# A mixture-of-experts kernel: expert outputs stored in the order of the units and gathered per token inside the expert loop

## The reference

```python
x = x + attn(layernorm(x))                          # token mixer, then channel mixer
xt = layernorm(x).reshape(-1, 256)                  # 8192 tokens
gates = sigmoid(xt @ expert_sel.T)                  # 8192 x 32
sel_val, sel_idx = top_k(gates, 4)
scores = relu(einsum('nd,edf->nef', xt, keys))      # 128 numbers per expert
scores = scores * gate_full[:, :, None]             # 0 where the expert was not taken
x = x + einsum('nef,efv->nv', scores, values)
```

## Time and profile before

| what | value |
|---|---|
| median of 3 runs | 1308.65 us (1304.46 to 1309.5) |
| span of the profiled execution, first to last instruction | 1307.0 us |
| mean granted TensorE clock | 0.966 of full |
| PE busy | 1185.3 us (91%) |
| DVE busy | 1030.5 us (79%) |
| ACT busy | 832.7 us (64%) |
| POOL busy | 800.2 us (61%) |
| DMA | 196.98 MB, mean 151 GB/s |

### The profile page before, as it was taken

How to read it: one execution, slowest core, us unless ns; L and a number is a source line. 1 busy time by engine, 2 the same in 40 slices (tenths; PEclk the granted TensorE clock), 3 DMA queues, 4 the chain that set the end, 5 groups by cost and what they waited for, 6 DMA issues and landing times.

```text
span 1307.0 us, 27473 instructions
## 1 busy us (share of the span) xinstructions
PE 1185.3 (91%) x7372; PEld 1030.4 (79%) x7373; DVE 1030.5 (79%) x2462; ACT 832.7 (64%) x1761; POOL 800.2 (61%) x900
## 2 busy tenths in 40 slices
PE   7799999999999999999999875999999999992665
PEld 6678887888788778887878754999999999992444
DVE  4789889888988887898898668777777777771777
ACT  4468567656856765675685562677777777771443
POOL 2523567666866866776675667677777777774000
PEclk9799999999999999999999985999999999995999
DMA  7001112121221212122121287787766666668999
GB/s 229 1 17 33 57 50 90 66 77 53 77 77 49 89 58 76 61 73 81 45 86 58 103 340 258 227 248 236 213 209 211 206 207 204 204 186 296 411 412 355
DMA packets 119841, 196.98 MB, mean 151 GB/s; under 512 B 16368, under 2 KB 92400, under 8 KB 118384
## 3 DMA queue, kind: packets, MB, share of 16 engines
q1 hardware_dynamic: 82672, 114.03, 27.3%
q0 software_dynamic: 26112, 71.86, 15.0%
q10 hardware_dynamic: 11008, 10.52, 2.3%
HBM read 101.09 MB, written 95.26 MB: 150 GB/s over the span
## 4 chain that ended last, share of the span: by engine, by line
PE 57%; DVE 9%; POOL 9%; DMA 8%; issue 8%; ACT 5%; SPq 2%; DVEq 1%; ACTq 0%; POOLq 0%
PE ps L468 18%; PE ps L1559 12%; DMA ye<-expert_rows_spare 5%; POOL lists L1351 4%; PE ps L1547 4%; PE ps L677 3%; PE ps L1540 2%; PE ps L671 2%; PE ps L673 2%; PE ps L1541 2%; PE ps L1542 2%; DMA expert_rows_spare<-y,dest 2%; PE ps L615 2%; ACT kr L770 1%; PE ps L458 1%
## 5 line engine op out<-in xcount | busy, mean ns | idle before, releaser
L1678 POOL DMA_INDIRECT expert_rows_spare<-y,dest x288 | 282.2, 980 | 92.8 <-issue 84.6
L1559 PE MATMUL ps<-xt_hi,keys 128*128 128x128 f32 x1152 | 223.7, 281 | 6.8 <-DVE keys L1628 6.8
L1559 PEld LDWEIGHTS ps<-xt_hi,keys 128*128 128x128 f32 x1152 | 188.2, 194 | 9.3 <-DVE keys L1628 8.8
L1351 POOL DMA_INDIRECT lists<-rows_even,slot x128 | 145.0, 1133 | 42.6 <-issue 38.1
L1351 POOL DMA_INDIRECT lists<-rows_odd,slot x128 | 140.5, 1098 | 41.1 <-issue 39.0
L1559 PE MATMUL ps<-xt_lo,keys 128*128 128x128 f32 x576 | 159.4, 277 | 0.0
L1639 DVE TENSOR_TENSOR xt_lo<-ps,xt_hi 128x512 fp32r<-128x512 f32 x144 | 99.5, 691 | 59.2 <-ACT xt_hi L1592 58.3
L1592 ACT ACTIVATE xt_hi<-ps 128x512 fp32r<-128x512 f32 x144 | 86.3, 599 | 84.6 <-PE ps L1559 79.2
L1628 DVE TENSOR_TENSOR keys<-experts_raw,keys 128x256 fp32r<-128x256 f32 x288 | 108.6, 418 | 14.2 <-issue 8.9
L1589 ACT ACTIVATE keys<-experts_raw 128x256 fp32r x288 | 105.4, 425 | 19.5 <-issue 19.3
L1763 PE MATMUL ps<-ye,gate_diag 128*128 128x256 f32 x256 | 66.1, 404 | 56.4 <-DMA ye<-expert_rows_spare 54.8
(11 more groups left out here) (235 smaller groups left out, 3409.0 us busy)
## 6 DMA issues: line engine op xcount, KB each, us to landing
xr<-lists SPq DMA_DIRECT2D x288, 130.0 KB
ye<-expert_rows_spare SPq DMA_DIRECT2D x32, 1024.0 KB, 21.8
x_sb<-in_x SPq DMA_DIRECT2D x16, 512.0 KB, 3.8
residual<-xp SPq DMA_DIRECT2D x16, 512.0 KB, 4.6
experts_raw<-in_expert_in SPq DMA_DIRECT2D x8, 1024.0 KB, 15.5
resid<-residual SPq DMA_DIRECT2D x4, 2048.0 KB, 13.3
out_dram<-resid ACTq DMA_DIRECT2D x32, 256.0 KB, 11.7
expert_rows_spare<-y,dest POOLq DMA_INDIRECT x288
```

The costliest lines, as they stand in the source:

```text
L1351: pool.indirect_dma_start(lists, bass.IndirectOffsetOnAxis(ap=slot[:, q, n:n + 1], axis=0), rows[q][:, n // TOPK, :], None).then_inc(last_ ...
L1559: mm = pe.matmul(ps[:, H + q % HBANKS, c], keys[:, q, s, half, k * DE:(k + 1) * DE], m[:, q, k, c], start=n == 0, stop=n == 3 * KD - 1)
L1678: pool.indirect_dma_start(expert_rows, bass.IndirectOffsetOnAxis(ap=dest[:, r, s:s + 1], axis=0), y[:, r, s, :], None).then_inc(sent[r], 16)
```

## The change

Units are numbered in the order in which they are opened, over all experts: unit `n` lies at row `128 n` of the lists, whichever expert it belongs to. `route_slots` keeps, for each expert, the end of its open unit and what room is left in it, and opens new units as they are needed; a row's place is so known with its final number, and `place_of` keeps the 4 x 512 places of each tile. A row has 256 numbers (1024 bytes). The lists, 36,864 rows, are cleared with zeros in the mix stage, 2048 rows per transfer; the fills of list ends and the plan of units go, but for a smaller plan (`plan_filled`, `plan_order`, `plan_head`, `plan_later`, `plan_end`): 16 units that are full before the last tile go first, then the others in order.

In the expert loop the products are stored by SP, 7 steps behind the loads, to `sorted_rows` at the unit's own rows. POOL waits until all units that a tile can lie in are stored (tile `t`: the first 8 (t + 3) steps), and gathers the rows of its tokens by `place_of`, 16 indirect transfers per tile, to `ye`. DVE sums the four rows of 128 tokens with their gates into `resid` from step 34 on, two instructions per step, between its other work; SP loads the residual and stores the output per tile of 512 tokens. The hardware loop repeats 16 steps. SP waits for `last_scattered` ahead of step 8. The last phase, with its matmuls, goes.

```diff
-ROW = D + TOPK
+ROW = D
...
+UNIT = P
 RING = 8
-
-UNIT = P
-EARLY = ((N - TILE) * TOPK - E * (UNIT - 1)) // UNIT // (SUB * RING) * RING
 UNITS = -(-((N * TOPK - E) // UNIT + E) // (SUB * RING)) * SUB * RING
+LIST = UNIT
+LIST_ROWS = UNITS * UNIT
+HEAD = SUB * RING
+HEAD_END = HEAD + E
+OPENED = TILE * TOPK // UNIT
+LAG_UNITS = E
...
+STORE_LAG, SUM_LAG = 7, 34
+OPEN_BELOW = (UNIT - 1) / UNIT
+EXPERT_SLOTS = (4, 2, 2, 4, 4, 2)
...
+    sorted_rows = nc.dram_tensor("sorted_rows", (LIST_ROWS, D), F32, kind="Internal").ap()
...
+        def clear(first):
+
+            sp.dma_start(lists[bass.ds(first, OPENED * UNIT), :].rearrange("(p n) d -> p n d", n=OPENED),
+                         zeros[:].unsqueeze(1).broadcast_to([P, OPENED, ROW])).then_inc(zeroed, 16)
+
+        AHEAD = LAG_UNITS // OPENED + 1
+        for n in range(AHEAD):
+            clear(n * OPENED * UNIT)
...
+            if has_next:
+                sp.wait_ge(zeroed, 16 * (t + AHEAD))
+                clear((t + AHEAD) * (OPENED * UNIT))
...
-            dve.scalar_tensor_tensor(rows[p][:, :, D:ROW], expert[:], float(SPACED), out_row[:],
-                                     ALU.mult, ALU.add).then_inc(route_step, 1)
-            after_route(5)
-            dve.tensor_scalar(out_row[:], out_row[:], float(TILE * TOPK), None, ALU.add)
...
-            dve.tensor_tensor(place[:], ps[:, PR, 0:J * E].rearrange("p (j e) -> p j e", j=J),
-                              list_end[:].unsqueeze(1).broadcast_to([P, J, E]),
-                              ALU.add).then_inc(place_ready, 1)
-            dve.wait_ge(place_ready, V + 1)
-            dve.tensor_tensor(list_end[:], ps[:, PR, J * E:(J + 1) * E], list_end[:],
-                              ALU.add).then_inc(rank_used, 1)
...
+            dve.tensor_tensor(count_i[:], ps[:, PR, J * E:(J + 1) * E], room[:], ALU.subtract).then_inc(units_step, 1)
+            dve.tensor_tensor(place[:], ranks, room[:].unsqueeze(1).broadcast_to(at),
+                              ALU.subtract).then_inc(rank_used, 1)
+            after_units(1)
+            dve.tensor_scalar(opened_i[:], count_i[:], UNIT.bit_length() - 1, None,
+                              ALU.logical_shift_right).then_inc(units_step, 1)
+            after_units(2)
+            dve.tensor_copy(opened[:], opened_i[:]).then_inc(units_step, 1)
+            after_units(3)
+            dve.tensor_tensor_scan(upto, zeros[:, 0:E], opened[:], before, ALU.add, ALU.add).then_inc(units_step, 1)
+            settled(rank_used, V + 1)
+            dve.scalar_tensor_tensor(room[:], opened[:], float(UNIT), count_i[:], ALU.mult, ALU.subtract)
+            after_units(4)
+            dve.tensor_tensor(fresh[:], upto, opened[:], ALU.subtract).then_inc(units_step, 1)
+            dve.scalar_tensor_tensor(newest[:], opened[:], 0.0, upto, ALU.is_gt, ALU.mult)
+            after_units(5)
+            dve.scalar_tensor_tensor(jump[:], fresh[:], float(UNIT), unit_end[:], ALU.mult,
+                                     ALU.subtract).then_inc(units_step, 1)
+            after_units(6)
+            dve.scalar_tensor_tensor(over[:], place[:], float(UNIT - 1), jump[:].unsqueeze(1).broadcast_to(at),
+                                     ALU.is_ge, ALU.mult)
+            dve.tensor_tensor(place[:], place[:], unit_end[:].unsqueeze(1).broadcast_to(at),
+                              ALU.add).then_inc(units_step, 1)
+            after_units(7)
+            dve.tensor_tensor(place[:], place[:], over[:], ALU.add).then_inc(place_ready, 1)
+            dve.scalar_tensor_tensor(unit_end[:], newest[:], float(UNIT), unit_end[:], ALU.mult,
+                                     ALU.max).then_inc(units_step, 1)
...
+            dve.tensor_copy(place_of[:, bass.ds(V * (J * TOPK), J * TOPK)], slot_f[:])
...
+            dve.wait_ge(head_counts, 4)
+            dve.tensor_copy(plan_expert[:, 0:P], ps[:, HEAD_BANK, P:2 * P])
+            dve.tensor_scalar(plan_row[:], ps[:, HEAD_BANK, 2 * P:2 * P + HEAD_END], float(UNIT), None,
+                              ALU.mult).then_inc(head_ready, 1)
...
+                settled_on(pool, zeroed, 16 * t)
...
+        def rows_of(b):
+            if isinstance(b, int) and b * SUB < HEAD_END:
+                _, at = nc.values_load_multi_w_load_instructions(
+                    plan_row[0:1, b * SUB:(b + 1) * SUB], engines=(sp.engine,), min_val=0,
+                    max_val=LIST_ROWS - UNIT,
+                    skip_runtime_bounds_check_because="the plan writes all of the table, bounded, ahead of head_ready")
+                return at
+            return [b * BLOCK + s * UNIT for s in range(SUB)]
+
+        def step(i, r, pair):
+            if within(i, 0, NSTEPS):
+                at = rows_of(i)
+                after(sp, x_ready, i - SLOTS + 1)
+                for s in range(SUB):
+                    sp.dma_start(xr[:, r % SLOTS, s, :], lists[bass.ds(at[s], UNIT), :]
+                                 ).then_inc(rows_loaded[r % SLOTS], 16)
+            if within(i, STORE_LAG, NSTEPS + STORE_LAG):
+                b, q = i - STORE_LAG, (r - STORE_LAG) % YS
+                at = rows_of(b)
+                sp.wait_ge(ycopy_ready, b + 1)
+                for s in range(SUB):
+                    sp.dma_start(sorted_rows[bass.ds(at[s], UNIT), :], y[:, q, s, :]).then_inc(y_stored[q], 16)
+            if r % RING == 6 and within(i, 46, NSTEPS):
+                tile, q = 2 * pair + (r - 46) // RING, ((r - 46) // RING) % RS
+                store_tile(tile, q)
+            if r % RING == 0 and within(i, 32, NSTEPS):
+                load_resid(2 * pair + (r - 32) // RING, ((r - 32) // RING) % RS, pair - 2)
+
+        def load_resid(tile, q, nth):
+
+            after(sp, out_stored[q], 16 * nth)
+            sp.dma_start(resid[:, q], residual[bass.ds(tile * TILE, TILE), :].rearrange("(j p) d -> p j d", p=P)
+                         ).then_inc(resid_loaded[q], 16)
+
+        def store_tile(tile, q):
+
+            sp.wait_ge(sum_step, TOPK * J * (tile + 1))
+            sp.dma_start(out[bass.ds(tile * TILE, TILE), :].rearrange("(j p) d -> p j d", p=P), resid[:, q]
+                         ).then_inc(out_stored[q], 16)
+
+        sp.wait_ge(head_ready, 1)
         sp.wait_ge(scattered[0], 16 * NT // 2 * J * TOPK)
         sp.wait_ge(scattered[1], 16 * (NT // 2 - 1) * J * TOPK)
-        for i in range(FILL_RINGS * RING):
+        for i in range(3 * PAIR):
             if i == RING:
-                sp.wait_ge(plan_ready, PLANNED)
-            step(i, i % RING, i // RING)
-            if i % RING == RING - 1:
-                fill(sp, i // RING * FILLS)
-        with sp.Fori(FILL_RINGS, EARLY // RING) as ring:
-            for r in range(RING):
-                step(RING * ring + r, r, ring)
-
-        sp.wait_ge(last_scattered, 16 * J * TOPK)
-        sp.wait_ge(filled, 16 * E)
-        sp.wait_ge(area_cleared, 16 * (LIST_ROWS - OVERFLOW) // UNIT)
-        with sp.Fori(EARLY // RING, NSTEPS // RING) as ring:
-            for r in range(RING):
-                step(RING * ring + r, r, ring)
-        sp.wait_ge(pe_step, LAST_STEP)
-        for n in range(RESID_AHEAD, RESID_PIECES):
-            load_resid(sp, resid, residual, resid_loaded[1], n)
+                sp.wait_ge(last_scattered, 16 * J * TOPK)
...
+        def add(i, r, pair, k):
+
+            if not within(i, SUM_LAG, SUM_END):
+                return
+            G, tile, q, j, nth = group(r, pair)
+            if r % 2:
+                k += 2
+            if k == 0:
+                dve.wait_ge(ye_loaded[j], 16 * TOPK * (tile + 1))
+                if j == 0:
+                    dve.wait_ge(resid_loaded[q], 16 * (nth + 1))
+            else:
+                dve.wait_ge(sum_step, TOPK * G + k)
+            acc = resid[:, q, j, :]
+            gate = gates[:, bass.ds(G, 1), k:k + 1].rearrange("p a b -> p (a b)")
+            dve.scalar_tensor_tensor(acc, ye[:, j, k, :], gate, acc, ALU.mult, ALU.add).then_inc(sum_step, 1)
...
+            add(i, r, pair, 0)
+            if within(i, 0, NSTEPS):
...
-                dve.tensor_tensor(mark[:, r, :, 0:TOPK], xr[:, q, :, D:ROW],
-                                  plan_mark[:, bass.ds(i * SUB, SUB)].unsqueeze(2).broadcast_to([P, SUB, TOPK]),
-                                  ALU.subtract).then_inc(mark_ready, 1)
...
+            add(i, r, pair, 1)
+            if within(i, H_LAG, NSTEPS + H_LAG):
...
-                dve.tensor_reduce(dest[:, r, :], mark[:, r], AX_X, ALU.min,
-                                  apply_absolute_value=True).then_inc(dest_ready, 1)
...
-            settled_on(pool, ycopy_ready, i + 1, dest_ready)
-            for s in range(SUB):
-                pool.indirect_dma_start(
-                    expert_rows, bass.IndirectOffsetOnAxis(ap=dest[:, r, s:s + 1], axis=0), y[:, r, s, :],
-                    None).then_inc(sent[r], 16)
...
+        for tile in range(NT):
+            for q in range(YS):
```

(70 more changed lines are left out.)

681 lines of the change are left out of this document (213 added, 468 removed).

## The result

The changed kernel takes 1296.37 us (median of 7, 1289.86 to 1304.96), the kernel before on the same chip 1306.94 (7): a ratio of 0.993 with a 95% interval of 0.990 to 0.996. It is faster by 0.7%, a small change but with an interval clear of 1, so the sign, forecast at 0.90, came out; the forecast of 1234 us and its range (1198 to 1272) did not. The profiled execution's span is 1294.4 us.

What follows compares the result with a forecast made beforehand. Bounds were taken as TensorE in the mix stage and expert loop, and DMA behind the loop. 1307 + 13 − 8 + 14 − 94 = 1232 us of span, forecast 1234 us, own range 1215 to 1255, full range 1198 to 1272.

Steps and rivals of the forecast that it cites:

- The last phase: From the opening of step 143 to the end: 133.1 us become 39, so −94 us (−98 to −80).
- The mix stage: Before the expert loop: a longer slot computation delays each tile by 1.0 to 1.1 us over 13 tiles, +13 us.
- the slot chain: Mix stage: seven short dependent DVE instructions in each tile's `route_slots` make `place` ready 2.6 us after they begin.
- rival of the whole chain coming through: Mix stage: all 2.6 us of each tile's added DVE instructions delay the kernel, +36 for +13, 1257 us; chance 0.12.
- The start of the loop: Up to step 8: plan instructions and fills go, SP waits for the last scatter; step 8 opens about 827, −8 us.
- SP issues four transfers a step instead of two; that is hidden, since SP only waits for buffers: Expert loop: SP's doubled transfers per step were claimed to add no time.
- The loop: Steps 32 to 143: 2.65 us a step over 111 steps, 294 us against 280, +14 us (−5 to +76).
- the store is issued three steps after the copy: Expert loop, y stores: hidden unless a store takes over 3 steps, though `y` buffers go from 8 to 4.
- 917.5 KB / 355 GB/s = 2.58 us: Expert loop, DMA time per step: 896 rows of 1024 B at the rate of a stretch behind the loop; bounds 2.24 and 3.2.
- rival with 65 ns a row: Expert loop: DMA takes 65 ns a row read, 3.2 us a step, +76, total 1296 us; chance 0.08.
- 1.75 − 0.14 + 0.80 = 2.41 us, or 2.57: Expert loop, DVE's turn: loses `mark` and the reduction, gains two sums; just under or just over TensorE's 2.475.
- POOL as the bound: Expert loop: rival in which every gather waits for one DVE sum, 3.5 us a step, +108 for +14, 1335 us; chance 0.08.

Runs made afterwards that it cites:

- e7: Changed kernel with each 2 MB of zeros of the mix stage written twice, the second time to an unread table: step 0 opens at 829.3 us, not 815.0.
- e9: Changed kernel with y stores one step later (lag 8) and SP's row numbers kept in registers: 1261.38 us, ratio 0.967 to the kernel before.
- e6: Changed kernel, lag 7, with SP's row numbers kept in registers from load to store: ratio 0.982 to the kernel before; steps 8 to 32 take 62.7 us.
- e1: Changed kernel with y stores issued one step later (lag 8 for 7): ratio 0.974 to the kernel before; steps 32 to 143 take 312.5 us.
- e2: Changed kernel, lag 7, without the gathers of tiles 1 to 15 (output wrong): steps 32 to 143 take 306.3 us, where the changed kernel takes 335.2.
- e5: Changed kernel with y stores one step later, and two of each token's four sums left out (output wrong): steps 32 to 143 take 310.1 us.
- e11: Changed kernel with later y stores and row numbers in registers, without gathers of tiles 1 to 15 and half the sums: steps 32 to 143 take 295.2 us.

## Why the prediction was wrong

**The last phase: right but for one step.** −94 forecast, −91.3 measured (41.8 us against 39). The gathers run at 0.95 + 0.30 us, the four sums at 0.5. "POOL is free by then" failed: POOL gathers without a pause from 1247.98 on, so the last tile's 16 gathers begin 15.9 us after the opening of step 143, not 10.7; landing and store were 0.6 and 0.7 us shorter than taken.

**The mix stage: size right by luck, place wrong.** +13 forecast, +11.3 measured at step 0. A tile takes 46.8 us in the median, 45.7 before, and e7 leaves the zeros out as a cause. The wait is not at TensorE's second transposes (0.3 us there): TensorE waits for `k_lo`, 14.3 us between 200 and 780 us where it was 6.1. One `k_lo` in each tile runs beside POOL's product `th_r`, before the change and after it:

```profile
349.96 3.33 POOL L1394 TENSOR_TENSOR th_r<-th_r,u 128x512 f32<-128x512 f32 x2 [1.17 <-DVE th_r L1055]
350.39 1.76 DVE L1017 TENSOR_TENSOR k_lo<-ksq,k_hi 128x512 fp32r<-128x512 f32 x1
```
```profile
401.88 3.42 DVE L990 TENSOR_TENSOR k_lo<-ksq,k_hi 128x512 fp32r<-128x512 f32 x1
402.23 2.52 POOL L1317 TENSOR_TENSOR th_r<-th_r,u 128x512 f32<-128x512 f32 x2
```

The median `k_lo` takes 0.69 us. Beside the product it took 1.76 in 12 tiles before and takes 3.42 in 11 tiles now, because POOL, which has a scatter to finish first (until 402.20), begins the product behind `k_lo` and not ahead of it. POOL also waits 19.6 us for `place` between 200 and 780 us, which is not among its waits before. So the slot chain seems to reach TensorE over POOL's order and this overlap, which the prediction does not have; no run takes the chain out to confirm it. Its own chain is also short of its figure: seven links of 0.3 and 0.28 are 2.4 us, not 2.6. The rival of the whole chain coming through (+36) is refuted.

**The start of the loop: wrong, −8 forecast, +12.1 measured.** Two steps failed. "Behind SP's wait stand all loads and stores; TensorE waits for them" priced SP's path, and that came out: step 8's load is issued at 834.42. But TensorE did not wait for it: it ran steps 0 to 4 at the lower clock. The windows around the change (columns as above):

```profile
830.00:834.00 4.00, 4.00 (x21) 4.00 (x21) 1.70 (x4) 1.97 (x5) 1.91 (x2) 0.50 0.40 146
834.00:838.00 4.00, 4.00 (x37) 4.00 (x37) 1.69 (x4) 2.55 (x7) 0.00 (x0) 1.00 0.40 130
```

It is granted 1.2 GHz until 834, 19 us after step 0 opens, after some 12 us with hardly a matmul. Busy 25.2 of 27.4 us, it is itself the bound there, and the 4 us forecast for steps 0 to 8 did not come (27.36 us, as before). In e9, where the clock is back at 2.4 GHz by 830, these steps take 24.9. The other step, "SP issues four transfers a step instead of two; that is hidden, since SP only waits for buffers", forgot that the stores of steps 0 to 23 each read the table again. e6 gives that its price: 12.2 us. The 3.4 us of the fills did not come either: e6 still takes 62.7 us, not 59.4; TensorE waits 2.2 us for rows there, the rest is open.

**The loop: wrong, +14 forecast, +55.3 measured.** First, 22.7 us of order, by e1. What failed is "the store is issued three steps after the copy". SP runs ahead: it issues step i's load once xt_lo of step i − 4 is done, and then, with a lag of 7, waits for the y copy of step i − 7, which ACT makes in step i − 3, a step later. So the next load stood behind a wait for the future, and behind each residual load SP could not make up the time. Second, 18.5 us of throughput (312.5 against 294). "917.5 KB / 355 GB/s = 2.58 us" took its rate from 13 us in which residual loads and scatters ran together; with everything in flight the full engines moved 325 to 329 GB/s, 2.79 to 2.82 us a step. The prediction's own sign, under 330 GB/s at a share of 1, came. By e1's queues a row of q1 costs 69.5% × 16 × 312.5 / (640 × 111) = 49 ns and a gathered one 54 ns, so the rival with 65 ns a row is not what happened, although its 1296 us is by chance the result. "1.75 − 0.14 + 0.80 = 2.41 us, or 2.57" for DVE's turn left out its gaps: 2.70 by e2's timeline. The two limits lie within 4%, so relieving one gained 2 us (e5 against e1) or 6 (e2, with a lag of 7, against e1), both 15 (e11 against e9). Why one gap in eight steps is 1 us, and why TensorE's matmuls in e11 take more than 2.475 us a step, stays open.

The Trainium skill (DMA: Bandwidth & Descriptors, Specifications) puts a core's HBM limit at about 358 GB/s. The loop stays below it by 30 GB/s with the engines at 1.00, and the earlier trace rows was above it; here neither this figure nor the 409 is the rate to plan with.

**POOL as the bound: refuted.** Gathers take 985 ns on average beside DVE's sums and 0.95 us in the tail. The Trainium skill (SBUF — State Buffer, Who interferes with whom) has DVE instructions with two SBUF inputs contend with GpSimd instructions that read SBUF; it also infers that making descriptors needs the write side, which would leave gathers out, so the prediction's "By it this rival would hold" went too far. The rows show next to none of it for gathers, and plainly for POOL's own product (`k_lo` above).

Forecast of the span and measurement: 1307 + 13 − 8 + 14 − 94 = 1232; 1307.0 + 11.3 + 12.1 + 55.3 − 91.3 = 1294.4.

## What to carry to other kernels

Where one queue issues both loads and stores in order, write down for each turn the event that each waits for, and in which step that event happens: a store that waits for a later step than the next load holds that load back, and one step more of lag was worth 23 us here, all of it behind the large loads in the same queue. Price a full DMA by a stretch with the same mix of directions and queues, not by a short one with some of it, and count the table reads of an issuing engine beside its transfers. When two limits lie within 5% of each other, an edit to one moves the time by a few us only: relieve both at once before calling one innocent.
